# Two convolution layers on one core: the shared sums of the last evictions made by ScalarE writes and accumulating DMAs in place of VectorE operations

## The reference

```python
# x: (8, 32, 64, 64) float32
x = x + L0(gn(x))     # a 3x3 and a 5x5 convolution; the 3x3 one, shifted nine ways, and the 5x5 one,
                      # weighted per channel and summed, with biases
x = x + L1(gn(x))     # patches of 3x3 with a leading 1, all products of two of the ten entries,
                      # times filters (32, 32, 10, 10), summed over channels and products
# gn: each channel of each image normalised by its own mean and variance
```

## Time and profile before

| | |
|---|---|
| time, median of 3 runs | 303.13 us (302.38 to 303.31) |
| profiled execution: span from first to last instruction | 300.4 us |
| its own device time | not listed apart; the median lies 2.7 us above the span |
| PE busy | 273.3 us (91%) |
| DVE busy | 252.8 us (84%) |
| ACT busy | 87.6 us (29%) |
| POOL busy | 29.0 us (10%) |
| mean granted clock of PE | 0.986 of full speed |

### The profile page before, as it was taken

The page is one execution under the profiler, slowest core; times in us unless marked ns, Lnnn a source line. Parts: engine busy times, 40 slices in busy tenths (PEclk is TensorE's granted clock), DMA queues, the critical chain, the costliest instruction groups (busy, mean ns, idle before and its releaser), DMA issues.

```text
span 300.4 us, 13567 instructions
## 1 busy us (share of the span) xinstructions
PE 273.3 (91%) x6464; PEld 130.6 (43%) x6464; DVE 252.8 (84%) x216; ACT 87.6 (29%) x135; POOL 29.0 (10%) x82
## 2 busy tenths in 40 slices
PE   0589999899999999999999999999999999999930
PEld 0224343344434433363546475344345446467310
DVE  1899899998999979799999999984999999970330
ACT  4532006979169789539000000004000000000000
POOL 7913920000110000000000000000000000000000
PEclk9999999999999999999999999999999999999995
DMA  6973000000000000000000000085000000000049
GB/s 190 382 203 82 4 2 3 2 5 2 2 2 4 4 2 4 2 2 3 4 2 4 2 4 4 2 171 115 2 2 4 2 2 4 2 4 4 2 91 189
DMA packets 19206, 11.45 MB, mean 38 GB/s; under 512 B 17744, under 2 KB 17872, under 8 KB 19024
## 3 DMA queue, kind: packets, MB, share of 16 engines
q1 hardware_dynamic: 14640, 9.06, 11.9%
q10 hardware_dynamic: 4512, 1.53, 2.2%
HBM read 6.40 MB, written 4.19 MB: 35 GB/s over the span
## 4 chain that ended last, share of the span: by engine, by line
PE 71%; DVE 15%; ACT 4%; issue 3%; DMA 2%; SPq 1%; DVEq 0%
PE acc L1007 63%; PE acc L1050 7%; ACT raw L507 3%; DMA raw<-in_x 2%; DVE stats L741 2%; DVE product L637 2%; DVE plane L759 2%; PE acc L1101 2%; DVE scaled L637 1%; DVE raw L801 1%; DVE product L872 1%; DVE product L663 1%; DVE product L669 1%; DVE arena L669 1%; DVE product L673 1%
## 5 line engine op out<-in xcount | busy, mean ns | idle before, releaser
L1007 PE MATMUL acc<-product,weight 32*32 32x512 f32 (+1 forms) x3072 | 126.8, 604 | 0.3 <-DVE product L872 0.3
L1007 PEld LDWEIGHTS acc<-product,weight 32*32 32x32 f32 (+1 forms) x3072 | 65.2, 110 | 59.4 <-issue 41.5
L879 DVE TENSOR_TENSOR product<-plane 128x4096 f32<-128x4096 f32 x19 | 83.3, 4430 | 0.1
L1007 PE MATMUL acc<-raw,weight 32*32 32x512 f32 (+1 forms) x960 | 45.4, 604 | 0.0
L1050 PE MATMUL acc<-product,middle 32*64 32x512 f32 (+1 forms) x576 | 30.2, 598 | 0.0
L1007 PEld LDWEIGHTS acc<-raw,weight 32*32 32x32 f32 (+1 forms) x960 | 20.7, 112 | 20.2 <-issue 15.7
L801 DVE TENSOR_TENSOR raw<-acc,arena 128x512 f32<-128x512 f32 x16 | 9.9, 683 | 16.7 <-issue 16.6
L1007 PE MATMUL acc<-product,arena 32*32 32x512 f32 (+1 forms) x448 | 22.2, 604 | 0.0
L879 DVE TENSOR_TENSOR raw<-plane 128x4096 f32<-128x4096 f32 x5 | 22.1, 4428 | 0.0
L741 DVE BATCH_NORM_STATS2 stats<-raw 128x6 f32<-128x512 f32 x32 | 19.7, 681 | 2.7 <-DMA raw<-in_x 2.6
L507 ACT ACTIVATE raw<-arena 32x512 f32<-32x512 f32 x32 | 21.8, 681 | 0.5
(11 more groups left out here) (121 smaller groups left out, 209.9 us busy)
## 6 DMA issues: line engine op xcount, KB each, us to landing
raw<-in_x SPq DMA_DIRECT2D x8, 512.0 KB, 8.3
out<-raw SPq DMA_DIRECT2D x24, 128.0 KB, 3.0
arena<-in_L_conv_filters SPq DMA_DIRECT2D x4, 400.0 KB, 6.9
out<-raw ACTq DMA_DIRECT2D x8, 128.0 KB, 4.7
arena<-in_L_conv_w ACTq DMA_DIRECT2D x4, 100.0 KB, 4.0
w_in<-in_L_conv_w ACTq DMA_DIRECT2D x2, 36.0 KB, 1.8
w_in<-in_L_conv_w SPq DMA_DIRECT2D x2, 36.0 KB, 2.2
b_in<-in_L_conv_b SPq DMA_DIRECT2D x2, 0.5 KB
```

The source lines that it names most:

```text
L879: nc.vector.tensor_tensor(both_halves(g, u), plane_halves(g), plane_halves(g, PRODUCTS[k][0] * PITCH + PRODUCTS[k][1]), ALU.mult)\
L1007: return nc.tensor.matmul(acc[32 * s:32 * (s + strips), j, r, :], weights[32 * r:32 * r + 32, t:t + strips, :] .rearrange("p t c -> p (t c ...
```

## The change

DVE no longer runs `mix`. Instead:

- ACT, in the new `put_cross(g)`, writes cross + offset to `even_shared` and offset - cross to a new range `odd_shared` (eight instructions of 128 x 512, four for each). `put_cross(0)` stands after `square(1)`, `put_cross(1)` after `keep_cross(1)`.
- POOL then issues for each group two DMAs from SBUF to SBUF that add `kept_sum` to `even_shared` and to `odd_shared` (`accum_op=ALU.add`, 128 x 2048 float32 each). They stand at the end of POOL's program. The kernel before issues no DMA from POOL.
- `evict` waits for the landing of the DMA of its half, `keep_sum(1)` for the landing of both DMAs of group 0; `put_cross(1)` waits for `evicted` 8.

```diff
+        odd_shared = arena[:, GROUP * CHUNK:2 * GROUP * CHUNK]
...
+            for g in range(NG):
+                pool.wait_ge(shared_kept, 2 * (g + 1))
+                pool.wait_ge(cross_put, 2 * g + 1)
+                pool.dma_start(even_shared, kept_sum, accum_op=ALU.add).then_inc(even_shared_ready[g], 16)
+                pool.wait_ge(cross_put, 2 * g + 2)
+                pool.dma_start(odd_shared, kept_sum, accum_op=ALU.add).then_inc(odd_shared_ready[g], 16)
...
             def keep_sum(g):
...
                 if g == 1:
+                    act.wait_ge(even_shared_ready[0], 16)
+                    act.wait_ge(odd_shared_ready[0], 16)
...
+            def put_cross(g):
+
+                act.wait_ge(shared_kept, 2 * (g + 1))
+                if g == 1:
                     act.wait_ge(evicted, 2 * GROUP)
...
+                for to, sign in ((even_shared, 1.0), (odd_shared, -1.0)):
+                    for r in range(GROUP):
+                        part = slice(CHUNK * r, CHUNK * (r + 1))
+                        last = nc.scalar.activation(to[:, part], kept_cross[:, part], ACT.Identity,
+                                                    bias=offset_by_strip[:, r, g:g + 1], scale=sign)
+                    last.then_inc(cross_put, 1)
...
             square(1)
+            put_cross(0)
             keep_sum(1)
             keep_cross(1)
+            put_cross(1)
...
-            def mix(g):
-
-                dve.wait_ge(shared_kept, 2 * (g + 1))
-                dve.wait_ge(offset_spread, 1)
...
-                for r in range(GROUP):
-                    last = nc.vector.scalar_tensor_tensor(image(even_shared, r), image(kept_sum, r),
-                                                          offset_by_strip[:, r, g:g + 1], image(kept_cross, r),
-                                                          ALU.add, ALU.add)
-                step(last)
-                for r in range(GROUP):
-                    last = nc.vector.scalar_tensor_tensor(image(kept_sum, r), image(kept_sum, r),
-                                                          offset_by_strip[:, r, g:g + 1], image(kept_cross, r),
-                                                          ALU.add, ALU.subtract)
-                last.then_inc(mixed, 1)
...
             def evict(g, odd):
-                dve.wait_ge(mixed, g + 1)
+                dve.wait_ge((odd_shared_ready if odd else even_shared_ready)[g], 16)
                 dve.wait_ge(half_done, 2 * g + odd + 1)
```

More of the change, by code:

```diff
@@ L217, in conv_kernel @@
         shared_kept = sem("shared_kept")
-        mixed = sem("mixed")
+        cross_put = sem("cross_put")
+        even_shared_ready = [sem(f"even_shared_ready{g}") for g in range(NG)]
+        odd_shared_ready = [sem(f"odd_shared_ready{g}") for g in range(NG)]
         half_done = sem("half_done")
@@ L535, in keep_sum @@
                 if g == 1:
-                    act.wait_ge(evicted, 2 * GROUP)
+                    act.wait_ge(even_shared_ready[0], 16)
+                    act.wait_ge(odd_shared_ready[0], 16)
                 nc.scalar.activation(kept_sum, part_acc(0), ACT.Copy).then_inc(shared_kept, 1)
@@ L541, in keep_cross @@
                 wait_used(act, g, SQUARE_MIXED)
+                nc.scalar.activation(kept_cross, part_acc(1), ACT.Copy).then_inc(shared_kept, 1)
+            def put_cross(g):
+                act.wait_ge(shared_kept, 2 * (g + 1))
                 if g == 1:
-                    act.wait_ge(mixed, 1)
-                nc.scalar.activation(kept_cross, part_acc(1), ACT.Copy).then_inc(shared_kept, 1)
+                    act.wait_ge(evicted, 2 * GROUP)
+                for to, sign in ((even_shared, 1.0), (odd_shared, -1.0)):
[4 more added lines that the diff above has]
+                    last.then_inc(cross_put, 1)
             def spread_offset():
@@ L798, in evict @@
                     dve.wait_ge(stored, 16 * GROUP * STRIPS)
-                shared = kept_sum if odd else even_shared
+                shared = odd_shared if odd else even_shared
                 for r in range(GROUP):
@@ L972, in _ @@
             multiply(0, 10)
-            mix(0)
             for u in range(11, LAST_UNIT + 1):
@@ L990, in _ @@
             next_right(1)
[L991 to L994, removed]
+            for u in range(7, LAST_UNIT + 1):
                 multiply(1, u)
```

## The result

The changed kernel takes 306.09 us (median of 4, 305.94 to 306.72), the kernel before 303.04 us in the same comparison (302.38 to 303.31). The ratio is 1.0119, with a 95% interval of 1.0091 to 1.0146.

What follows compares the result with a forecast made beforehand. PE was taken to bound layer 1 with one 173.68 us piece; the DVE, ACT, DMA and POOL terms were all 0, so span 300.4 us plus 2.7 gave 303.1 us, range 302.0 to 305.0.

Steps and rivals of the forecast that it cites:

- The reading of the windows: Layer 1, units 7 to 17: PE takes 61.84 us in group 0, 61.83 in group 1, so DVE doesn't hold it.
- the rival by which PE follows DVE: Layer 1: PE is held back by DVE's products; 292.2 us at full price, 302.3 in mild form; chance 0.06.
- The estimate of 4.4 us for a plain copy: New DMAs: 2.0 us plus bytes over 436,000 per us, for a plain copy of 1.05 MB.
- All deadlines: Additions wanted by the evictions at 187.79, near 194, 281.93 and 287.89 us, and by `keep_sum(1)` at 202.69.
- the rival of the late DMA: Evictions or `keep_sum(1)` wait for an addition, and PE behind them; 324 us at the upper bound; chance 0.03.
- the halving of before: DVE operation at 37.34 us took 4.30 us beside POOL's additions, 2.28 without; basis for POOL slowing DVE, chance 0.04.
- The rule that I had set beside it: VectorE with two SBUF inputs contends with GpSimd reading SBUF, not only writing; descriptor writing would cost DVE nothing.
- The rival of a price around the span: First POOL-issued DMA costs time before the first or after the last instruction; up to 305.8 us; chance 0.10.
- The 2.7 us that the prediction carried over: Whole kernel: the median's distance above the span of 300.4 us, added to give 303.1 us.
- + 0 (DMAs): Term of the sum for the four accumulating DMAs of 1.05 MB: 0 us added to the span.
- the part on POOL and the DMA engines: The four additions in layer 1, taken at 10 us each, land before they are wanted: 0 us on the path.

Runs made afterwards that it cites:

- the four chained beside before: Kernel before, `mix` kept, plus four accumulating 1 MB DMAs from POOL into a spare range, each issued when the last has landed: 304.89 us, ratio 1.0077.

## Why the prediction was wrong

**Right.** PE sets the end of layer 1, and what DVE gets back is worth nothing: 173.70 us of PE with `mix` gone against 173.68 with it. The reading of the windows held, and the rival by which PE follows DVE is out for these stretches. ACT's writes cost 5.00 us where 5.6 were worked out, beside other work. The additions were taken at 10 us each and landed after 10.1. In part that is luck: the 10.1 are for two issued together, and one alone landed after 8.2 us (the four chained beside before). The estimate of 4.4 us for a plain copy was low: two issued together landed after 6.1. All deadlines were met with 30 us and more to spare, so the rival of the late DMA is out. DVE wasn't slowed by POOL's issues, four products in 17.48 us with them and without; the halving of before was the effect of additions on POOL itself and said nothing about issuing a DMA. The rule that I had set beside it (the Trainium skill, SBUF — State Buffer, Who interferes with whom) fits this. The rival of a price around the span named up to 305.8 us, near the result, but for a reason that the runs exclude: 0.3 us of the 3 lie around the span, and the run without any DMA from POOL has them too, while the four DMAs beside the kernel before don't. The 2.7 us that the prediction carried over were a median less the span of another execution; of one and the same execution it is 1.7 to 1.8 us.

**Wrong.** The step that failed is the sum's "+ 0 (DMAs)", and in the part on POOL and the DMA engines the inference from "With 10 us each, even one after another, they have landed by 165 and by 233" to "Cost on the path 0". It asked who waits for the landing of the new DMAs. It never asked who else uses the engines on which they run. The page listed that user, `q8 instruction`, with 50 packets, and the chain showed PE in one piece of 173.68 us, an engine that uses up 0.82 MB of instructions over the run and has only what has been fetched ahead to live on. Measured, the term is 2.66 us in place of 0. With the 0.3 us around the span that makes the 3 us by which the kernel got slower.

**How firmly.** Shown by runs: the DMAs alone cost the time (304.89 beside an unchanged kernel, 303.38 without them), no traffic in SBUF is needed, nor an addition, and the same additions in small pieces with pauses cost nothing. That the link is the instruction fetch is shown by the traces of six kernels with stops: a packet of `q8` starts late, PE stops in front of the first instruction of that packet, and nowhere else in layer 1, and goes on 1.2 to 1.6 us after its landing. I have no run in which the fetches alone were changed. Left open: why a fetch gets no turn for 4 us though it has a queue of its own, and whether a long transfer issued by another engine than GpSimd does the same.

## What to carry to other kernels

A DMA off the path isn't free because nobody waits for it. Where one engine runs without a pause through thousands of short instructions, its own instruction stream is a DMA with a deadline of a few us, and a large transfer beside it can make it late. Here two copies of 1 MB (engines held for 7.6 us) were covered and two additions of 1 MB (11.7 us) were not; between them it depends on how much lead the packet in question has. If such a transfer is needed, cut it in pieces and wait for each landing before the next is issued: pieces of 256 KB were free here, pieces of 1 MB were not. And before work is moved off a busy engine, compare the same stretch where it is loaded and where it isn't: here that alone said that there was nothing to win.

## What the hardware showed that I had not expected

An accumulating DMA in SBUF holds the engines half as long again as a copy of the same size: a pair 11.7 us against 7.6, with 0.64 us against 0.32 (median) for a packet of 8 KB. Stops of PE by its instruction stream appear in the chain as "issue" with no releaser, and only in part: 1.17 us of 2.66. They can be told by their place: always at the same instructions, 256 or a multiple of it apart. Cutting a transfer into smaller descriptors helps little if all of them are queued at once (305.37 us). Waiting between whole transfers of 1 MB helps in part (304.37 us), and both together remove the loss (303.01 us).
